# Laying attention numerators over stored denominators by DMA, with the gate put on the values by ScalarE

## The reference, cut to what matters

```python
def _L0_xattn_ref(q, k, v, gamma):          # q: layernorm(x), k = v = ctx, all [16, 128, 512]
    qh = q.reshape(B, h, dq, Lq)            # h = 8 heads, dq = 16
    kh = k.reshape(B, h, dq, Lk)
    vh = v.reshape(B, h, dv, Lk)
    qk = jnp.einsum('bhdq,bhdl->bhql', qh, kh) * scale
    sm = jax.nn.softmax(qk, axis=-1)
    ret = jnp.einsum('bhql,bhdl->bhdq', sm, vh)
    return gamma * ret.reshape(B, Dv, Lq)

x = x + jnp.tanh(g_xattn[0]) * _L0_xattn_ref(_layernorm(x), ctx_2048, ctx_2048, L0_xattn_gamma)
x = x + jnp.tanh(g_ffn[0]) * _L0_ffn_ref(_layernorm(x), ...)   # router, top 2 of 8 experts, shared expert, core path
```

## Time and profile before

| | |
|---|---|
| median of 3 runs | 714.83 us (714.03 to 716.48) |
| profiled execution, its own time | 716.26 us |
| span of the profiled execution | 714.4 us |
| TensorE busy | 662.5 us (93% of the span) |
| ScalarE busy | 531.0 us (74%) |
| VectorE busy | 512.4 us (72%) |
| GpSimd busy | 464.7 us (65%) |

### The profile page before, as it was taken

The page is one execution under the profiler, slowest core; times in us unless marked ns, Lnnn a source line. Parts: engine busy times, 40 slices in busy tenths (PEclk is TensorE's granted clock), DMA queues, the critical chain, the costliest instruction groups (busy, mean ns, idle before and its releaser), DMA issues. The chain is left out here.

```text
span 714.4 us, 20683 instructions
## 1 busy us (share of the span) xinstructions
PE 662.5 (93%) x6005; PEld 352.7 (49%) x6005; DVE 512.4 (72%) x859; ACT 531.0 (74%) x1125; POOL 464.7 (65%) x464
## 2 busy tenths in 40 slices
PE   1798998899999999999999998879999999999998
PEld 0122222233333233322345554448999999998744
DVE  4988999899999999999878665564444444444456
ACT  2398998799999999999888467448777777677411
POOL 3557698888889888886846713404566665675622
PEclk9999999999999999999999999989999999999999
DMA  6646575656666566565334652448989779677587
GB/s 201 212 139 192 181 237 155 216 179 205 207 222 193 180 214 204 183 193 169 125 117 160 218 182 104 164 110 148 189 111 137 122 121 131 94 115 98 58 274 269
DMA packets 128176, 120.15 MB, mean 168 GB/s; under 512 B 64100, under 2 KB 97636, under 8 KB 128104
## 3 DMA queue, kind: packets, MB, share of 16 engines
q1 hardware_dynamic: 114680, 104.09, 50.1%
q0 software_dynamic: 12192, 14.16, 12.8%
q10 hardware_dynamic: 1232, 0.98, 0.4%
HBM read 60.25 MB, written 49.10 MB: 153 GB/s over the span
## 5 line engine op out<-in xcount | busy, mean ns | idle before, releaser
L716 DVE TENSOR_REDUCE mx<-nat 128x2 f32<-128x1024 f32 x256 | 296.6, 1213 | 24.3 <-PE nat L545 23.2
L641 ACT ACTIVATE P<-ring 128x512 f32<-128x512 f32 x512 | 279.4, 603 | 20.4 <-PE ring L557 10.4
L2229 POOL DMA_INDIRECT y_sums<-ysb,to x74 | 124.4, 1681 | 91.9 <-DVE ysb L2163 74.1
L570 PE MATMUL pv<-P,VT 128*32 128x256 f32 x2048 | 159.1, 395 | 0.4
L545 PE MATMUL nat<-KS,QS 48*128 48x512 f16 x512 | 111.9, 398 | 25.8 <-DMA QS<-q_scratch 15.0
L557 PE MATMUL ring<-QS,KS 49*128 49x512 f16 x512 | 123.5, 393 | 8.6 <-ACT P L641 8.6
L1331 PE MATMUL EH<-XA,whi 128*128 128x256 f16 (+1 forms) x688 | 104.5, 258 | 0.0
L1331 PE MATMUL Y<-whi,u 128*128 x592 | 104.0, 273 | 0.1
L570 PEld LDWEIGHTS pv<-P,VT 128*32 128x32 f32 x2048 | 44.1, 109 | 92.5 <-issue 44.6
L2113 DVE TENSOR_TENSOR u<-X,u 128x512 f16<-128x512 f32 x62 | 42.7, 689 | 64.6 <-ACT u L1737 64.6
L557 PEld LDWEIGHTS ring<-QS,KS 49*128 49x128 f16 x512 | 32.2, 93 | 111.7 <-ACT P L641 94.7
(11 more groups left out here) (282 smaller groups left out, 1033.4 us busy)
## 6 DMA issues: line engine op xcount, KB each, us to landing
XA<-in_wall SPq DMA_DIRECT2D x8, 800.0 KB, 4.4
u<-in_wall SPq DMA_DIRECT2D x8, 800.0 KB, 4.4
QS<-q_scratch SPq DMA_DIRECT2D x64, 96.0 KB, 2.5
KS<-k_scratch SPq DMA_DIRECT2D x62, 96.0 KB, 2.2
X<-in_x SPq DMA_DIRECT2D x16, 256.0 KB, 2.8
q_scratch<-qhl SPq DMA_DIRECT2D x16, 256.0 KB, 2.1
xr<-in_x SPq DMA_DIRECT2D x16, 256.0 KB, 3.6
rd<-den_scratch SPq DMA_DIRECT2D x16, 256.0 KB
```

Source lines behind the costliest of these rows:

```text
L570: m = pe.matmul(pv[32 * j:32 * j + 32, q], VT[i][:, lb, g, j, :], Pb[4 * (s % 2) + j][:, q], start=(lb == 0 and half == 0), stop=(lb == 3) ...
L641: act.activation(Pb[4 * (s % 2) + j][:, :], bank[:, :], ACT.Exp).then_inc(t_use.sem, 1)
L716: dve.tensor_reduce(mx[:, k // 8, :, k % 8], nat[k % 2][:, :, :], AX.X, ALU.max).then_inc(t_max.sem, 1)
L2229: pool.indirect_dma_start(out=ysum[:, :], out_offset=bass.IndirectOffsetOnAxis(ap=to[:, j % 2, a:a + 1], axis=0), in_=ysb[j % 2][:, a, :], ...
```

## The change

The gate moves from the sums to the values: ScalarE writes `VT` with `act.mul(..., gate[:, 5:6])`, a scale that it reads from a column of SBUF, where it copied before. The ones are not scaled, so the denominators stay as they were. The masks go: after SP has stored the denominators, four DMAs of 16 rows by 512 (32 KB each, SBUF to SBUF) lay the numerator rows of `U[1]` over the denominator rows of group 0's sums, and `att` multiplies that tile by `rd` directly. `na`, `nb`, `num` and the tile `cme` go. Group 0's sums alternate between `U[0]` and the former `tn`; `U[1]` is free again when the four DMAs have landed (semaphore `t_nm`).

```diff
+    t_nm = T("numerators_in", 16)
+    totals = lambda b, g: U[1] if g else (U[0], tn)[b % 2]
...
     def pool_jobs(w):
         jobs = []
-        if 2 <= w < B + 2:
-            jobs += [(w - 2, n) for n in ("na", "nb", "num")]
...
-                    sp.dma_start(sd[ck.index(t), 0].rearrange("(j g) q -> g j q", g=2)[g], U[g][r:P:32, :]).then_inc(t_ds.sem, 16)
+                    sp.dma_start(sd[ck.index(t), 0].rearrange("(j g) q -> g j q", g=2)[g], totals(t, g)[r:P:32, :]).then_inc(t_ds.sem, 16)
...
                 ck.wait(t_pool, t - 1, "x1")
+                for r in range(DH, P, 32):
+                    sp.dma_start(totals(t, 0)[r:r + DH, :], totals(t, 1)[r:r + DH, :]).then_inc(t_nm.sem, 16)
                 sp.dma_start(xr[:, :], x[ck.index(t)]).then_inc(t_xr.sem, 16)
...
         def value_sums(ck, b, s):
             ck.wait(t_pv, b, s)
-            ck.wait(t_pool, b - 1, "nb")
-            ck.wait(t_ds, b - 1)
-            act.copy(U[s // 4][:, :], pv[:, :]).then_inc(t_ev.sem, 1)
+            if s // 4:
+                ck.wait(t_nm, b - 1)
+                ck.wait(t_ds, b - 1)
+            else:
+                ck.wait(t_pool, b - 2, "att")
+            act.copy(totals(b, s // 4)[:, :], pv[:, :]).then_inc(t_ev.sem, 1)
...
+                    if (w, a) == (0, 0):
+                        act.wait_ge(t_gate.sem, 2)
                     src = bank[:, 0:2 * P].rearrange("p (l j g d) -> p l g j d", l=2, g=2, d=DH)
                     for g in range(2):
-                        m = act.copy(VT[i][:, 2 * a:2 * a + 2, g, :, DH * g:DH * g + DH], src[:, :, g, :, :])
+                        m = act.mul(VT[i][:, 2 * a:2 * a + 2, g, :, DH * g:DH * g + DH], src[:, :, g, :, :], gate[:, 5:6])
...
-            if what == "na":
-                ck.wait(t_ev, b, 1)
-                ck.wait(t_pool, b - 1, "att")
-                done(pool.tensor_scalar(tn[:, :], U[0][:, :], cme[:, 0:1], 1.0, ALU.mult, ALU.mult))
-            elif what == "nb":
+            if what == "att":
+                ck.wait(t_rb, b)
+                ck.wait(t_nm, b)
                 ck.wait(t_st, b - 2)
-                done(pool.tensor_scalar(ao[i][:, :], U[1][:, :], cme[:, 1:2], 1.0, ALU.mult, ALU.mult))
-            elif what == "num":
-                ck.wait(t_pool, b, "nb")
-                done(pool.tensor_tensor(tn[:, :], tn[:, :], ao[i][:, :], ALU.add))
-            elif what == "att":
-                ck.wait(t_rb, b)
-                ck.wait(t_pool, b, "num")
-                done(pool.tensor_tensor(ao[i][:, :], tn[:, :], rd[:, :], ALU.mult))
+                done(pool.tensor_tensor(ao[i][:, :], totals(b, 0)[:, :], rd[:, :], ALU.mult))
```

More of the change, by code:

```diff
@@ L261, in attention @@
     tn = A("tn", [P, L])
-    cme = A("cme", [P, 2])
     dc, rc = A("dc", [P, NH * L // P]), A("rc", [P, NH * L // P])
@@ L369, in attention @@
             t_ds.plan(w - 2, n=2)
+            t_nm.plan(w - 2, n=P // 32)
             t_rb.plan(w - 2)
@@ L824, in body @@
                 pool.tensor_tensor(gate[:, 5:6], gate[:, 3:4], gate[:, 2:3], ALU.mult).then_inc(t_gate.sem, 1)
-                pool.wait_ge(t_gate.sem, 2)
-                pool.tensor_scalar(cme[:, 0:2], cst[:, K_ME:K_ME + 2], gate[:, 5:6], None, ALU.mult).then_inc(t_gate.sem, 1)
-                pool.wait_ge(t_gate.sem, 3)
         def last_norm():
@@ L876, in free_sums @@
     def free_sums(eng):
-        eng.wait_ge(t_pool.sem, t_pool.at[B - 1, "nb"])
+        eng.wait_ge(t_nm.sem, t_nm.value)
         eng.wait_ge(t_ds.sem, t_ds.value)
```

## The result

| | before | after |
|---|---|---|
| median | 714.74 us (714.03 to 716.48) | **726.18 us** (725.0 to 727.29) |
| ratio, 95% interval | | **1.0157** (1.0116 to 1.0197) |
| span of the profiled execution | 714.4 us | 725.0 us |

The kernel became 1.57% slower, 11.4 us. The forecast was 718.0 and its range ended at 721.8.

What follows compares the result with a forecast made beforehand. VectorE was taken to pace the window, except at the values' copies, where TensorE and ScalarE do. Terms 0 + 2.4 + 0.4 + 0.4 = +3.2 us on the median 714.83 gave 718.0 us; range 714.4 to 721.8.

Steps and rivals of the forecast that it cites:

- What bounds the kernel: Steady window of 20.71 us: VectorE paces it, except where TensorE and ScalarE do, at the first two copies of VT.
- Three GpSimd operations go: GpSimd, each window: 2.66 us of work removed, splits 2.7 us sooner, worth 0 on the path.
- The gate's read: ScalarE's copies into VT: reading the gate delays the first bank by 0.18 us a window, 2.4 us over 13 windows.
- Four DMAs on SP: SP's queue: 2.02 us of issues a window, absorbed by vanished waits for GpSimd's splits and by cover; steady cost 0.
- The slack: SP's waits a window: 1.3 us for the keys' split, 0.7 for the queries' split, 0.47 for ScalarE's sums.
- The cover of 0.9 us: SP's queue: 0.47 us at its window's end plus 0.46 us to spare in the load of `dc`, at least.
- Windows 4 and 5: Reciprocal there already waits for `dc`, so no cover for SP's issues: 0 to 1 us for both, taken at 0.4.
- The last batch: SP's end of batch 15: added issues make `rd`, `att`, `x1` 0.8 us later; bounds 0 and 0.8, taken at 0.4.
- SP becomes the bound: Rival, chance 0.12: the four transfers delay the keys' landing beyond cover, 0.4 us in 14 windows, 723.6 us.
- Its sign, VectorE waiting for `dc`: Reciprocal on VectorE: waiting for `dc` in windows past the fifth would show the forecast wrong.

Runs made afterwards that it cites:

- e4: Changed kernel without the four DMAs, so the even-and-odd merge is left out: 715.66 us, ratio 1.0030.
- e3: Kernel before with only the gate moved to the values, GpSimd's three operations kept with masks without the gate: 715.44 us, ratio 1.0021.
- e1: Changed kernel with the values copied plainly, the gate left out of the result: 725.24 us, ratio 1.0182.
- e7: Changed kernel with four more DMAs of the same size, to a DRAM buffer nobody reads: 754.07 us, ratio 1.0558.
- e6: Changed kernel with only two of the four DMAs, half of the merge left out: 716.89 us, ratio 1.0046.
- e8: Kernel before with four added SP issues to a DRAM buffer, GpSimd's operations kept, values copied plainly: 721.03 us, ratio 1.0092.
- e11: Changed kernel with the four DMAs issued by GpSimd, behind the queries' split: 705.84 us, ratio 1.0054.
- e9: e5 with GpSimd's two splits of the expert part put ahead of its gate operation: 704.04 us, ratio 1.0029.
- e10: e9 with the last three batches' four issues moved behind the store of the reciprocals: 704.29 us, ratio 1.0039.
- e5: e2 with the values copied plainly and the gate multiplied onto `rd` by one GpSimd operation ahead of `att`: 723.83 us, ratio 1.0123.
- e2: Changed kernel with the same four DMAs issued behind the keys' store, except in the last three windows: 716.36 us, ratio 1.0036.
- e12: Changed kernel with the keys' store issued ahead of the four DMAs, `xr` and ctx: 704.10 us, ratio 1.0037.

## Why the prediction was wrong, step by step

*What bounds the kernel.* Right: TensorE and VectorE do the same work in the same time, and the first two copies of VT hold the chain at their place.

*Three GpSimd operations go, worth 0.* Right for the path: GpSimd waits 2.7 us a window for the statistics of x1, as foretold, and e4, level with e3, shows that their absence wins nothing. But this same step fed the next one, where it failed.

*The gate's read, 0.18 us a window.* Right in every number that the forecast gave: 368 ns (0.37), 1.14 us (1.13), a pause of 0.95 us (0.94), and in e3, where it stands alone, windows of 20.90 (20.9). For the whole kernel e3 measured 1.5 us where the sum had 2.4; the interval reaches to 2.9. The pointer's read added 89 ns of duration and (1.14 - 0.368) / 3 - 0.163 = 0.094 us of spacing, so the half of the two-operand row was a good price. The Trainium skill, page "ScalarE: Activation LUTs", section "What ACT_TABLE_LOAD costs", has about 93 ns for it, and the trace agrees. In the changed kernel, though, this term is not in the steady window at all: SP sets it, and e1 without the read has the same 21.40 us.

*Four DMAs on SP, steady cost 0.* This is the step that failed: "The keys' store used to wait 1.3 us for GpSimd; that wait goes", "The queries' split waited 0.7 us more; that goes too", "So the steady cost is 0". Four of its terms were off. Two lines of SP's list before (180 to 305 us) that the earlier trace rows do not have:

```profile
SPq L116 <- DMA k_scratch<-khl: 9.0, 6, 1.7
SPq L116 <- PE ring L589: 2.0, 6, 0.4
```

- The issues take 2.5 us, not 2.02. The nearest row was a store to DRAM; a copy from SBUF to SBUF takes 0.62 us per issue and one to DRAM 0.49, in one and the same window of e7.
- The landing of the keys was taken as unchanged, at nothing. SP's wait for it grew from 1.5 us a window (9.0 / 6) to 2.2 (10.9 / 5), so 0.7 of the 1.3 us came back as landing. The growth does not need the four DMAs: the wait is 1.5 and 1.7 us in the two profiles where the store comes 1.9 us behind the load of ctx (before, e3), and 2.2 to 2.7 us in the six where it comes 0.65 us behind (after, e1, e4, e6, e8, e11). Whether the distance is the cause or something that goes with it stays open.
- The slack was counted without one entry: 0.33 us a window of waiting for TensorE's transposes (2.0 / 6).
- The cover of 0.9 us was half of it no cover. The 0.46 us that `dc` had to spare pays for one delay. But SP's queue is a round, and what its issues exceed it by comes again in every window.

With the measured terms the sum reads as follows. SP had 1.3 + 0.7 + 0.47 us and 0.33 us to give up: 2.8 us. It got 2.5 us of issues and 0.7 us of landing, 3.2 us. The excess is 0.4 us a window; with the smaller entries (all waits on the two lists together, each divided by its count, fell from 5.0 to 3.1 us a window, so by 2.0; the issues and that of `xr` grew by 2.6) it is 0.6. Measured are 21.40 - 20.71 = 0.69 us, in e1 without the gate's read as in the changed kernel. By this count the issue alone set right, 2.5 against 2.8 us, would still have cost nothing: the growth of the landing is what took the sum over the edge.

The dose agrees: 1.2 us of issues cost nothing beyond the gate's read (e6), 1.9 us cost 0.33 us a window (e8), 2.5 us cost 0.69 (e1), and 2.14 us more cost 2.25 more (e7). As an estimate from these four, beyond about 1.6 to 1.8 us of issues each further us is about a us of window.

*Windows 4 and 5, taken at 0.4 us.* The direction was right, the size was not: the wait for `dc` in window 4 grew by 0.55 us, and the clock fell behind it. That window cost 3.6 us in the profiled execution. But the change cannot be charged with it on one profile. e9 and e10 are the same program up to window 14, and their window 4 took 25.50 us at a granted clock of 0.87 in one and 21.27 us at 1.00 in the other; the wait for `dc` ahead of it was 1.96 and 0.56 us. The granted clock in the same window is 0.86 to 0.93 in after, e1, e5, e7, e8 and e9, 0.96 in e6, and 1.00 in e2, e3, e4, e10, e11 and e12. The two pauses of TensorE ahead of `nat` add up to 2.1 us in after, 2.6 in e1, 1.9 in e8, 2.7 in e9, but to 1.5 in the kernel before and 0.9 in e10. In e5 they add up to 0.9 only and the clock is 0.92, so the pauses do not settle it. Of the timed executions the mean granted clock is on record: 0.981 to 0.990 in the six of e1, 0.990 to 0.998 in the 29 of the kernel before beside them, 0.992 to 0.998 in the twelve of e2. In e8 it is 0.986 to 0.990, against 0.990 to 0.997 beside it. So where SP's round sets the window the clock is lower in the timed executions too; but it also is in e5 (0.985 to 0.995), whose windows are short. What share of the 11.4 us the clock makes is not shown.

*The last batch, taken at 0.4 us.* `att` of batch 15 comes 74.9 us after the last statistics of x, before 74.1; the whole rest of the kernel is 1.8 us longer. SP's part was sized about right: the four issues took 3.27 us there, and the store of the reciprocals came 1.2 us later behind `dc` (0.8 foretold). But e10 wins nothing by moving them, so they are hardly the reason for the 1.8 us. What is, stays open.

*The rivals.* "SP becomes the bound" is what happened, and its price of 723.6 is 2.6 us below the result. Its condition named the wrong quantity: it watched the bytes of the four transfers, and what decided was the time of their issue. So its chance of 0.12 came from the 0.65 us of transfer, which e2 shows to be harmless, and that its price came near is luck: 0.4 us in 14 windows was worked out from a slower transfer. Its sign, VectorE waiting for `dc`, did come, in five of seven steady windows. The Trainium skill's rule on small transfers (page "DMA: Bandwidth & Descriptors", section "Measured (HBM→SBUF, 128 partitions, SWDGE, issued from GpSimd)"), which stood beside that rival, speaks of the transfers' own time; e2 and e12 make all four transfers a window and come to 1.0036 and 1.0037, against 1.0021 and 1.0030 without them (e3, e4), which is within the intervals.

Sum of what happened, in the profiled execution: the first eight windows 4.3 us (3.6 of them window 4), the seven steady ones 4.8 us, the rest 1.8 us, less 0.25 us because the first statistics start earlier: 10.6 us, the difference of the spans. The recorded range ends at 721.8 where its own sum gives 721.6; that changes nothing.

## What to carry to other kernels

A queue that issues DMAs and then waits for them to land is a round. Before adding to it, list all that it waits for in a window: only waits for other engines are slack, waits for its own landings are length, and a slack that you free by moving a store earlier may come back as a longer landing. Small DMAs are paid for at the issuer, one by one, here at 0.5 to 0.6 us each; put them where the queue waits for a landing anyway (e2, e12), or on an engine that idles (e11), and count who is queued behind.

And removing work from an engine that nobody waits for, here 17.5 us in seven windows, is worth nothing, so even the best form of this change came back to the start but for 0.3%.

## What the runs showed that was not expected

- The issue of a 32 KB copy takes 0.62 us on SP when the target is SBUF and 0.49 us when it is DRAM, from the same source in one window (e7), and no longer when the four stand at the first place (e8, 1.90 us for four).
- The keys' first store lands in 2.2 us (median of all windows) when it is issued 1.9 us behind the load of ctx (before), and in 3.0 us when it follows 0.65 us behind (e4). In e3, however, with SP's order as before, the median is 2.8 us as well, so the distance alone does not settle it.
- The same program had a window of 21.27 us in one profile (e10) and of 25.50 us in another (e9), the longer one at a granted clock of 0.87. One profile does not price such a window.
